# The last routed layer with f16 weight pairs, a token table and rows written in place

## The reference, cut to what matters

```python
def _L3_ffn_ref(x, gate_w, w1, b1, w2, b2):      # x: layernorm of the stream
    x_flat = x.reshape(-1, D)                    # 2048 tokens of 256
    router_probs = softmax(x_flat @ gate_w)      # 8 experts
    expert_idx = argmax(router_probs)
    expert_w = router_probs[expert_idx]
    for e in range(8):
        h = gelu(x_flat @ w1[e] + b1[e])         # 256 -> 1024
        y = h @ w2[e] + b2[e]                    # 1024 -> 256
        out = out + where(expert_idx == e, expert_w, 0)[:, None] * y
x = x + _L3_ffn_ref(_layernorm(x), ...)
```

## Time and profile before

| | us |
|---|---|
| median of 3 runs | 3392.41 |
| lowest and highest | 3390.27, 3396.36 |
| span of the profiled execution | 3394.3 |
| PE busy in it | 2924.9 (86%) |
| DVE, ACT, POOL busy | 2079.7, 1901.4, 1309.9 |
| routed layer m3, norm and routing | 3129 to 3187 |
| its 23 expert tiles | 3187 to 3361 |
| its combining | 3361 to 3394.3 |

### The profile page before, as it was taken

The page is one execution under the profiler, slowest core; times in us unless marked ns, Lnnn a source line. Parts: engine busy times, 40 slices in busy tenths (PEclk is TensorE's granted clock), DMA queues, the critical chain, the costliest instruction groups (busy, mean ns, idle before and its releaser), DMA issues. The chain is left out here.

```text
span 3394.3 us, 68325 instructions
## 1 busy us (share of the span) xinstructions
PE 2924.9 (86%) x26680; PEld 2032.0 (60%) x26681; DVE 2079.7 (61%) x3111; ACT 1901.4 (56%) x2879; POOL 1309.9 (39%) x944
## 2 busy tenths in 40 slices
PE   6769998746979998979998597979999999998596
PEld 3246665425546666546666596766666666667595
DVE  6968887577968873968783223855444444466222
ACT  3448886283658884658884112856555555466131
POOL 2259998020247884148883212820000000055212
PEclk8979998878989998989998798979999999998698
DMA  4611111200022220022222512011000000052612
GB/s 140 230 56 55 54 57 58 91 13 13 1 58 55 54 47 15 1 60 54 54 47 85 174 36 53 2 38 43 26 26 26 26 26 1 1 116 65 215 36 70
DMA packets 218053, 193.21 MB, mean 57 GB/s; under 512 B 126837, under 2 KB 176866, under 8 KB 216738
## 3 DMA queue, kind: packets, MB, share of 16 engines
q1 hardware_dynamic: 210247, 172.30, 17.6%
q0 software_dynamic: 5280, 14.42, 1.3%
q10 hardware_dynamic: 2233, 2.39, 0.2%
HBM read 112.72 MB, written 39.00 MB: 45 GB/s over the span
## 5 line engine op out<-in xcount | busy, mean ns | idle before, releaser
L2663 POOL TENSOR_TENSOR lta_p_lo<-lta_p,lta_p_hi 128x1024 f16<-128x1024 f32 x256 | 539.2, 2133 | 218.0 <-DVE lta_p_hi L2786 218.0
L2858 ACT ACTIVATE lta_p<-lta_banks,lw_gmax 128x512 f32<-128x512 f32 x512 | 324.0, 683 | 112.5 <-PE lta_banks L2701 108.0
L2769 DVE TENSOR_REDUCE lta_s_ps<-lta_s_ps 128x1 f32<-128x1101 f32 x240 | 314.3, 1309 | 106.4 <-PE lta_s_ps L2680 106.4
L3948 PE MATMUL m_h_ps<-m_x,m_w 128*128 128x512 f16 x1536 | 354.5, 381 | 3.5 <-issue 3.5
L3960 PE MATMUL m_y_ps<-m_w,m_hT 128*128 128x256 f16 x3072 | 355.8, 273 | 1.3 <-DVE m_hT L4118 1.3
L4118 DVE TENSOR_TENSOR m_hT<-m_h,m_hT 128x512 f16<-128x512 f32 x256 | 177.0, 692 | 277.6 <-ACT m_hT L4045 275.9
L4045 ACT ACTIVATE m_h<-m_h_ps,m_h_bias,m_h_scale 128x512 f32<-128x512 f32 x256 | 199.3, 779 | 261.6 <-PE m_h_ps L3948 253.4
L3960 PEld LDWEIGHTS m_y_ps<-m_w,m_hT 128*128 128x128 f16 x3072 | 299.2, 98 | 64.3 <-issue 7.1
L1242 POOL TENSOR_TENSOR c0a_tri_p_lo<-c0a_tri_p,c0a_tri_p_hi 128x1024 f16<-128x1024 f32 (+2 forms) x192 | 285.7, 1521 | 58.5 <-DVE c0a_tri_p_hi L1416 57.4
L3948 PEld LDWEIGHTS m_h_ps<-m_x,m_w 128*128 128x128 f16 x1536 | 150.9, 98 | 160.9 <-issue 7.6
L1491 ACT ACTIVATE c0a_tri_p<-c0a_banks,c_size 128x512 f32<-128x512 f32 (+3 forms) x384 | 208.6, 577 | 45.6 <-PE c0a_banks L1310 32.9
(11 more groups left out here) (771 smaller groups left out, 6594.8 us busy)
## 6 DMA issues: line engine op xcount, KB each, us to landing
m_w<-in_L_ffn_w_dram SPq DMA_DIRECT2D x4, 8192.0 KB, 40.4
m_raw<-in_L_ffn_W_dram SPq DMA_DIRECT2D x16, 1024.0 KB, 6.6
lta_q<-ltb_qT SPq DMA_DIRECT2D x96, 128.0 KB, 2.4
c_side<-in_fside_Bx16xSxS_dram SPq DMA_DIRECT2D x16, 616.0 KB, 4.9
c0a_tri_q<-c_near SPq DMA_DIRECT2D x96, 96.0 KB
c0a_tri_k<-c_mixed SPq DMA_DIRECT2D x93, 96.0 KB
lta_k<-ltb_kT SPq DMA_DIRECT2D x64, 137.6 KB, 2.5
lt_vh<-ltb_v SPq DMA_DIRECT2D x64, 128.0 KB
```

The lines of the kernel that those rows point to most:

```text
L2663: nc.gpsimd.tensor_tensor(p_lo[:, slot, :], p32[:, p32_slot(h, j), :], p_hi[:, slot, :], ALU.subtract).then_inc(rested, 1)
L2769: nc.vector.tensor_reduce(ntop_of(h)[:, n:n + 1], scores(h, n), AX_X, ALU.max, negate=True).then_inc(top_ready, 1)
L2858: nc.scalar.activation(p32[0:rows, slot, c * 512:(c + 1) * 512], t_ps[0:rows, c, :], ACT.Exp, bias=bias, scale=p["gmax"][0:rows, 0:1]).the ...
L3948: last = nc.tensor.matmul(h_ps[:, f % RING, :], w1[:, v, a, c, f * P:(f + 1) * P], x16[:, b, c, n * CHUNK:(n + 1) * CHUNK], start=c == 0 a ...
```

## The change

1. **Weights as pairs, made in the gated layer.** A new `PairWeights` object does for the routed layer's eight experts what the gated layer does for its own: load (now from POOL's queue), largest magnitude, scales, high half, low half. The pairs are stored in DRAM, one 1 MB matrix pair at a time. The steps are put between those of `gated_experts`, one routed expert beside each gated one; one `split_weights` of the gated layer moves from `k % 4 == 2` to `k % 4 == 1`.
2. **Routing by a token table.** The normalized row, the row of `x` and the token's weight (513 numbers) go to a table `rows` in token order, by plain transfers. PE and DVE compute `ids`: for each of 23 x 128 slots, the token that sits in it; empty slots repeat the expert's last token. All first matrices (8 MB of pairs) are loaded at once on ACT's queue. The 16 scatters of rows are gone. Norm, gates and routing are one block.
3. **Expert tiles.** POOL fetches the 128 rows of a tile by `ids` into a ring of three; three are fetched ahead of the loop. The second matrix comes tile by tile into a ring of three on SP. Products are three f16 matmuls each. DVE applies scale, bias, token weight and residual, and POOL scatters the finished rows straight to the output. `combine_experts` is gone.
4. One of two early stores of zeros to a `sorted_x` (3 MB) is gone.

The core of the diff:

```diff
+    def halve(self, act, e, k):
+        if k == 0:
+            act.wait_ge(self.sized, PairWeights.SIZES * e + PairWeights.SIZES)
+            act.wait_ge(self.pair_free, e + 1)
+        self.nc.scalar.activation(self.pair[k][:, 0, :], self.raw[k][:], ACT.Identity, scale=self.down[:, k:k + 1]).then_inc(self.halved, 1)
...
+XS_RING, W2_RING = 3, 3
...
+def gather_rows(nc, pool, r, j):
+    k = j % XS_RING
+    nc.gpsimd.indirect_dma_start(r["xs"][:, k, :], None, r["rows"],
+                                 bass.IndirectOffsetOnAxis(ap=r["ids"][:, j:j + 1], axis=0)).then_inc(r["xs_loaded"][k], 16)
...
+        sp.dma_start(by_tile[:, :, D:2 * D], env.x[:]).then_inc(x_stored, 16)
+        sp.dma_start(r["b2"][:], w("b2").partition_broadcast(P)).then_inc(r["b2_loaded"], 16)
+        for g in range(TILES // 4):
+            sp.wait_ge(normed, 4 * (g + 1))
+            sp.dma_start(by_tile[:, 4 * g:4 * g + 4, 0:D], xn[:, 4 * g:4 * g + 4, :]).then_inc(rows_stored, 16)
+        sp.wait_ge(weighted, 1)
+        sp.dma_start(by_tile[:, :, 2 * D:2 * D + 1], weight[:].unsqueeze(2), allow_slow_non_contiguous=True).then_inc(w_stored, 16)
...
+        act.dma_start(r["w1"][:], pairs.dram[0].rearrange("e p n -> p e n")).then_inc(r["w1_loaded"], 16)
...
+    @block.sync
+    def _(sp):
+        for j in range(W2_RING, NT):
+            sp.wait_ge(y_done, j - W2_RING + 1)
+            load_reduction(nc, sp, pairs, r, j)
+
+    @block.gpsimd
+    def _(pool):
+        for j in range(NT):
+            if j:
+                pool.wait_ge(ys_stored[(j - 1) % 2], 16 * ((j + 1) // 2))
+            pool.wait_ge(y_evac, j + 1)
+            nc.gpsimd.indirect_dma_start(out, bass.IndirectOffsetOnAxis(ap=r["ids"][:, j:j + 1], axis=0),
+                                         ys[:, j % 2, :], None).then_inc(ys_stored[j % 2], 16)
+            if j + XS_RING < NT:
+                gather_rows(nc, pool, r, j + XS_RING)
...
+        def turn(j):
+            u, k = j % 2, j % XS_RING
+            pe.wait_ge(r["xs_loaded"][k], 16 * (j // XS_RING + 1))
...
+        turn(0)
+        turn(1)
+        expand(0)
+        for j in range(NT):
+            if j + 2 < NT:
+                turn(j + 2)
+            if j + 1 < NT:
+                expand(j + 1)
+            reduce(j)
...
+        for j in range(NT):
+            split_h(j, 0)
+            if j:
+                combine(j - 1)
+            split_h(j, 1)
+            if j + 2 < NT:
+                split_x(j + 2)
+                copy_w(j + 2)
+        combine(NT - 1)
...
+        reduce_tops(0)
+        routed.load(pool, 0)
+        for e in range(E):
+            if e + 1 < E:
+                reduce_tops(e + 1)
+            routed.reduce_tops(pool, e)
+            routed.store(pool, e)
+            if e + 1 < E:
+                routed.load(pool, e + 1)
+            pool.wait_ge(routed.stored, 32 * (e + 1))
+            pool.sem_inc(routed.pair_free, 1)
...
+                    if k % CHUNKS == 2 and q < 2:
+                        routed.halve(act, 2 * i + k // CHUNKS, q)
...
-                    if more and k % CHUNKS == 2 and q < 2:
-                        split_weights(e, ev, q)
+                    if k % CHUNKS == 1 and q == 1:
+                        if not last and k < CHUNKS:
+                            dve.wait_ge(routed.bias_loaded, 16)
+                        routed.largest(dve, 2 * i + k // CHUNKS, 0)
+                    if k % CHUNKS == 1 and q == 2:
+                        routed.largest(dve, 2 * i + k // CHUNKS, 1)
+                        routed.largest(dve, 2 * i + k // CHUNKS, 2)
+                    if k % CHUNKS == 1 and q == 3:
+                        if more:
+                            split_weights(e, ev, 0)
+                        routed.sizes(dve, 2 * i + k // CHUNKS)
+                    if more and k % CHUNKS == 2 and q == 0:
+                        split_weights(e, ev, 1)
+                    if k % CHUNKS == 2 and q > 1:
+                        routed.split(dve, 2 * i + k // CHUNKS, q - 2)
```

More of the change, by code:

```diff
@@ L3269, in combine_experts, with paired_routed_stage @@
+ROW = 2 * D + 1
+XS_RING, W2_RING = 3, 3
+def paired_routed_stage(nc, env, tag, name, args, func, capacity, pairs, out):
+    w = lambda n: args[f"{name}_{n}"]
     with ExitStack() as ctx:
         st = Stage(nc, ctx, tag)
-        yg = st.sb("yg", [P, TILES, D])
-        gathered = env.gathered.pop()
-        added, stored = st.sem("added"), st.sem("stored")
-        block = ctx.enter_context(nc.Block())
-        @block.sync
-        def _(sp):
-            rows = out.rearrange("b (t p) d -> p (b t) d", p=P)
-            for t in range(TILES):
-                sp.wait_ge(added, t + 1)
-                sp.dma_start(rows[:, t, :], env.x[:, t, :]).then_inc(stored, 16)
-            sp.wait_ge(stored, 16 * TILES)
@@ L3284, in _ @@
-        @block.gpsimd
-        def _(pool):
-            for t in range(TILES):
-                nc.gpsimd.indirect_dma_start(yg[:, t, :], None, sorted_y, bass.IndirectOffsetOnAxis(ap=slot[:, t:t + 1], axis=0)
-                                             ).then_inc(gathered[t], 16)
-        @block.vector
-        def _(dve):
-            for t in range(TILES):
-                dve.wait_ge(gathered[t], 16)
-                nc.vector.scalar_tensor_tensor(env.x[:, t, :], yg[:, t, :], weight[:, t:t + 1], env.x[:, t, :], ALU.mult,
-                                               ALU.add).then_inc(added, 1)
-            dve.wait_ge(added, TILES)
+        r = {}
@@ new lines, in paired_routed_stage @@
+        r["rows"] = nc.dram_tensor(f"{tag}_rows", [T, ROW], F32).ap()
+        r["w1"], r["w2"] = st.sb("w1", [P, E, 2 * DC * F], F16), st.sb("w2", [P, W2_RING, 2 * FC * D], F16)
+        r["b2"] = st.sb("b2", [P, E, D])
+        r["xs"] = st.sb("xs", [P, XS_RING, ROW])
+        r["ids"], r["expert_of"] = st.sb("ids", [P, NT], U32), st.sb("expert_of", [P, NT], I32)
+        for n in ("h_in", "h_down", "y_back"):
+            r[n] = st.sb(n, [P, NT])
+        r["xs_loaded"] = [st.sem(f"xs_loaded{k}") for k in range(XS_RING)]
@@ new lines, in paired_routed_stage @@
+        r["w2_loaded"] = [st.sem(f"w2_loaded{k}") for k in range(W2_RING)]
+        r["w1_loaded"], r["b2_loaded"] = st.sem("w1_loaded"), st.sem("b2_loaded")
+        with ExitStack() as inner:
+            route_rows(nc, env, Stage(nc, inner, tag + "r"), inner, w, capacity, pairs, r)
+        with ExitStack() as inner:
+            paired_experts(nc, env, Stage(nc, inner, tag + "e"), inner, func, pairs, r, out)
+def gather_rows(nc, pool, r, j):
+    k = j % XS_RING
+    nc.gpsimd.indirect_dma_start(r["xs"][:, k, :], None, r["rows"],
+                                 bass.IndirectOffsetOnAxis(ap=r["ids"][:, j:j + 1], axis=0)).then_inc(r["xs_loaded"][k], 16)
@@ L3920, in _ @@
         sp.dma_start(b2[:], w("b2")).then_inc(b_loaded, 16)
+        routed.load_bias(sp)
         pairs(sp, pair)
@@ L3929, in _, with reduce_tops @@
                                 pattern=[[1, E], [-1, E]], channel_multiplier=0).then_inc(lower_made, 1)
-        for e in range(E):
+        def reduce_tops(e):
             pool.wait_ge(topped, 3 * e + 3)
```

388 lines of the change are left out of this document (378 added, 10 removed).

## The result

| | before | after |
|---|---|---|
| time, median (lowest to highest) | 3393.7 us (3390.3 to 3396.4) | 3559.2 us (3557.5 to 3562.4) |
| ratio, 95% interval | | 1.0489 (1.0477 to 1.0501) |
| span of the profiled execution | 3394.3 us | 3556.5 us |

The forecast was 3481 us, range 3430 to 3540. The direction was right, the time lies 78 us above the forecast and 19 above the range. The span grew by 162.2 us where the sum said 89, so 73 us are missing in the sum; the other 5 are the distance from a span to the median of the runs (the forecast took a median 1.9 us under the span; after, it lies 2.7 over it).

What follows compares the result with a forecast made beforehand. PE was taken to bound the expert tiles. Terms of -37.5 + 123 + 44 - 12.5 - 28 gave +89 us on the 3394.3 us span, 3483; the median lies 1.9 lower, so 3481 us, range 3430 to 3540.

Steps and rivals of the forecast that it cites:

- PE work in the tiles: Expert tiles: PE work per tile falls from 7.24 to 5.66 us with f16 products, -37.5 us in all.
- wait in every tile: Expert tiles: PE idles 6.15 us before a transpose until rows are fetched, 20 times, +123 us.
- clock: Expert tiles: PE loses its clock in each wait, 2.2 us each, 20 times, +44 us.
- ahead of the tiles: From routing to the first expert product: scatters go, table writes come, product at about 3178.4 instead of 3190.9, -12.5 us.
- end: After the last second product: combine, one scatter and its landing, 5 us instead of 33, -28 us.
- the rival without the clock loss (3437): Expert tiles: PE waits for fetched rows but keeps its clock; 3437 us, chance 0.11.
- the one in which the clock never returns (3550): Expert tiles: PE's clock stays low throughout the loop, +5.66 x 20 instead of 44; 3550 us, chance 0.08.
- The rival of open weight loads: Tiles' first products: PE weight loads no longer hide, 2.0 us more a tile, +46 in all; 3527 us, chance 0.03.
- The hidden fetch: Expert tiles: no wait before the transpose, so the sum is -78 us; 3314 us, chance 0.07.
- The late landing: Expert tiles: fetched rows land after 5.6 us, wait 8.4 us, 168 instead of 123; 3526 us, chance 0.10.
- The gated layer: Weight pairs made beside the gated experts: added DVE, ACT and POOL work is covered by PE, cost 0.

Runs made afterwards that it cites:

- the products in the gap: Against the kernel after, 50 extra products with unread results put ahead of each of the 20 turns that wait for fetched rows: 3517.5 us.
- The padding: Against the kernel after, table rows padded from 513 to 640 values (pitch 2560 bytes), the weight written as 128 copies: 3516.0 us.
- the last experiment in the tiles: Against the kernel after, POOL issues the next fetch of rows ahead of the scatter instead of behind it: 3535.7 us.
- The late turn: Against the kernel after, PE transposes tile j+2's rows behind the first product of tile j+1 instead of ahead of it: 3510.2 us.

## Where the prediction held and where it failed

| term | forecast | measured | from |
|---|---|---|---|
| PE work in the tiles | -37.5 | -38.4 | 132.0 us of tiles with five buffers, against 170.4 |
| wait in every tile | +123 | +142.4 | PE's waits |
| clock | +44 | +40.8 | 315.2 - 132.0 - 142.4; 38.1 by the products in the gap |
| ahead of the tiles | -12.5 | +40.2 | 3231.04 against 3190.88 |
| end | -28 | -22.7 | 10.3 us against 33 |
| sum | +89 | +162.3 | spans: +162.2 |

**The step that failed** is "Sum: ahead of the tiles": "The column of 2048 single weights queues behind 5 MB on SP while 8 MB of first matrices stream in; 13.4 MB at the 345 GB/s of this stage end near 3169." It names the right queue and the right last write, and it prices them by a rate that belonged to other transfers. The scatters of the earlier trace rows, the nearest to a write of rows in that trace, went into rows of 1024 bytes on a 1024-byte pitch. The new rows have a pitch of 2052 bytes, and writing them ran at about 91 GB/s with nothing else but a bias load beside it. The padding shows that this was all: with no fewer bytes, in the same order and on the same queue, the fetch starts at 3169.9 to 3171.4, where the step had put it. Of the miss of 52.6 us, 49.6 are the fetch's start (3218.6 instead of 3169). The other 3.1 are the way from there to the first product, 12.5 us instead of 9.4, of which the step had named 5.8, for three fetches and a barrier; the profile has 3.7 for the fetches, 6.2 from them to the first turn and 2.6 from there to the product. The bounds of this term, -17 and -5, came from no row that bore on a write at such a pitch, and without a row they should have been wide. The ids themselves, at 3166.4, were foreseen at 3167. Of the 73 us missing in the sum, 52.7 are this step's, 19.4 the wait's and 5.3 the end's; the clock and PE's work give 4.1 back. Had this step alone been wrong, the time would have come to 3534, inside the range, and with this step right and the others as they were to 3506.5. So it took more than one error to leave the range, and this was the largest.

**The wait** was the right mechanism, a little too small: 20 times, 7.1 us on average instead of 6.15. The hand-over from DVE to POOL took 0.82 where 0.31 was read off, in 19 of the 20 tiles. In the first, where POOL has no earlier scatter's landing to wait for ahead of the combination, it took 0.29, and with the fetch ahead of that wait (the last experiment in the tiles) 0.27 in all; that the second wait costs the half us fits, and was not tried by itself. The fetch itself came in 3.45 (median), as taken (3.4). Two of the 20 waits are over 9 us, with fetches that took 5.4 and 5.9.

**The clock** was right in mechanism and size. The granted clock is 0.74 over the tiles, and it falls in the gaps. After gaps of 4.0 us and more the products ran slow as after 6.8, after gaps of at most 3.1 (four buffers) they did not, and 50 products in the gap brought the clock to 0.98. That settles the rival without the clock loss (3437) and the one in which the clock never returns (3550): the latter's time is near the measured one for a wrong reason. The Trainium skill, TensorE: Matmul & The Clock Gate, section HAM oscillation, tells of transfer waits of 3 to 5 us that throw every burst back to the slow clock; these runs agree for gaps of 4.0 us and more, while those of 2.8 to 3.1 us with four buffers cost nothing.

**PE's work** was right to 1 us over all tiles. At full clock the 48 products of 128 columns take 2.84 us with their tail, (2.84 - 0.22) / 47 = 0.056 us apart. The rival of open weight loads has fallen with that. The 81 ns of the Trainium skill (TensorE: Matmul & The Clock Gate, section Back-to-back issue gap) would make them 3.9 us; the measurement decides, and here it is 2.84.

**The hidden fetch.** The rival said 3314 if the wait were gone and the rest of the sum held. Five buffers are that case: 3370.2. Of the difference of 56 us, 48 lie ahead of the tiles (first product at 3226.3 instead of 3178.4) and 5 at the end. With the padding too it is 3330. So the mechanism was priced rightly; the kernel after was not this case. The late turn shows that part of a cover gives part of the wait back, but nothing of the clock while 4 us remain.

**The late landing** (3526) did not occur: 3.4 us in the median. **The gated layer** costs nothing, as forecast; its cover was named and holds.

**The end** takes 10.3 us instead of 5. The last scatter starts 2.0 us after the last product, and 8.3 us pass from its start to the end of the span, where 3.5 were counted. The landing is 3.1 of these. In the 5.2 us behind it neither an engine nor a transfer is busy in the profile; the sum had nothing for them, and what they are stays open.

## What to carry to other kernels

A buffer ring is judged by the chain that releases it: here combination, scatter, fetch and landing take 6.8 us against 5.7 us of work a tile, and a ring of three, with its fetch released directly ahead of the reader, hides none of it, one of four most, one of five all but 2 us. When rows are laid out in DRAM for a gather, make the pitch and the ends of the pieces multiples of 64 bytes; one value too many a row cost 40 us and more here, while 2048 single 4-byte values at a pitch of 2112 bytes cost at most some 4. A rate read off one transfer prices another only if sizes and starts of the pieces are alike, and a busy share near 1 says nothing of bytes: read the GB/s beside it.
